# Order of TensorE's work in an attention kernel: both slots' scores ahead of the products with the values, in quads whose scores are corrected by VectorE

## The reference

```
q, k, v = n @ Wq, n @ Wk, n @ Wv              # n = layernorm(x)
latent = (k + v) @ W_down_kv
k_rec, v_rec = latent @ W_up_k, latent @ W_up_v
scores = clip(qh @ kh.T / (sqrt(128) + 1e-8))  # per head, 1024 x 1024
scores = clip(scores * exp(-0.0001 * |i - j|))
out = softmax(scores) @ vh
x = x + out @ Wo
x = x + (float8(layernorm(x)) @ float8(kernel)) * scales + bias
```

## Time and profile before

| | us |
|---|---|
| median of 3 runs (526.9, 526.92, 529.14) | 526.92 |
| the profiled execution's own time | 526.96 |
| its span, first to last instruction | 525.2 |
| TensorE (PE) busy | 487.2 (93%) |
| ScalarE (ACT) busy | 489.5 (93%) |
| VectorE (DVE) busy | 276.8 (53%) |
| GpSimd (POOL) busy | 218.9 (42%) |

### The profile page before, as it was taken

One profiled execution on the slowest core, in us unless ns is written; L12 is line 12 of the kernel. 1 busy time (PEld: TensorE's weight loads), 2 busy tenths in 40 slices (PEclk: granted clock), 3 DMA queues, 4 the chain that ended last, 5 costly groups with the idle time before them and its releaser, 6 DMA issues.

```text
span 525.2 us, 9404 instructions
## 1 busy us (share of the span) xinstructions
PE 487.2 (93%) x3457; PEld 111.9 (21%) x3457; DVE 276.8 (53%) x641; ACT 489.5 (93%) x534; POOL 218.9 (42%) x285
## 2 busy tenths in 40 slices
PE   8799999999999999999999999999999999999961
PEld 3312111122122122122121211122121212121220
DVE  5524554556654654546645565454654564445646
ACT  3789999999999999999999999999999999999961
POOL 0889519791630249982450219993101121002110
PEclk9999999999999999999999999999999999999995
DMA  5589989947994103667976001747987000100000
GB/s 178 166 258 227 325 190 198 338 179 175 258 207 105 46 7 143 210 229 171 249 166 150 8 5 61 275 165 208 259 168 182 8 4 7 47 0 2 1 21 25
DMA packets 50467, 73.79 MB, mean 140 GB/s; under 512 B 6192, under 2 KB 29168, under 8 KB 50416
## 3 DMA queue, kind: packets, MB, share of 16 engines
q1 hardware_dynamic: 49600, 72.85, 50.5%
q10 hardware_dynamic: 816, 0.28, 0.2%
HBM read 35.40 MB, written 35.65 MB: 135 GB/s over the span
## 4 chain that ended last, share of the span: by engine, by line
PE 55%; ACT 31%; issue 7%; DVE 6%; DVEq 0%; ACTq 0%
ACT probs L760 30%; PE ps L960 27%; PE ps L944 16%; DVE ps L1183 3%; PE ps L828 2%; PE ps L824 2%; PE ps L940 2%; PE ps L833 1%; PE ps L861 1%; PE ps L856 1%; PE ps L799 1%; PE ps L868 0%; DVE xn L1231 0%; PE ps L818 0%; DVE stats L1099 0%
## 5 line engine op out<-in xcount | busy, mean ns | idle before, releaser
L760 ACT ACTIVATE probs<-ps 128x1024 f32<-128x1024 f32 x512 | 478.9, 1061 | 9.7 <-DVE ps L1183 6.1
L960 PE MATMUL ps<-probs,V 128*9 128x512 f32 x2048 | 267.8, 594 | 3.2 <-ACT probs L760 0.8
L1183 DVE TENSOR_TENSOR ps<-ps,consts 128x256 f32<-128x256 f32 (+1 forms) x256 | 144.3, 566 | 173.1 <-PE ps L944 166.0
L944 PE MATMUL ps<-Qs,Ks 64*128 64x512 bf16 x992 | 179.1, 385 | 13.8 <-ACT probs L760 7.2
L944 PEld LDWEIGHTS ps<-Qs,Ks 64*128 64x128 bf16 x992 | 42.7, 93 | 281.5 <-ACT probs L760 265.9
L960 PEld LDWEIGHTS ps<-probs,V 128*9 128x9 f32 x2048 | 31.3, 88 | 80.3 <-issue 60.4
L564 POOL TENSOR_SCALAR rs<-mv 128x4 f32<-128x4 f32 (+1 forms) x10 | 2.3, 229 | 102.7 <-DVEq L1365 102.2
L1191 DVE COPY pv_out<-ps 105x512 f32<-105x512 f32 x31 | 21.4, 692 | 33.9 <-PE ps L960 33.9
L647 POOL TENSOR_TENSOR xs<-xs,magic 128x512 f32<-128x512 f32 x7 | 8.9, 1277 | 70.4 <-DVE magic L1244 70.4
L598 POOL TENSOR_TENSOR sq<-sq,parts 128x1024 f32<-128x1024 f32 (+1 forms) x16 | 28.4, 1773 | 1.3
L600 POOL TENSOR_TENSOR parts<-sq,parts 128x1024 bf16<-128x1024 f32 (+1 forms) x16 | 28.3, 1771 | 1.3
(11 more groups left out here) (148 smaller groups left out, 281.4 us busy)
## 6 DMA issues: line engine op xcount, KB each, us to landing
Qs<-qp_dram SPq DMA_DIRECT2D x26, 512.0 KB, 9.5
qp_dram<-parts SPq DMA_DIRECT2D x14, 768.0 KB, 5.2
Ks<-kp_dram SPq DMA_DIRECT2D x26, 384.0 KB, 6.0
kp_dram<-parts SPq DMA_DIRECT2D x12, 384.0 KB, 3.6
kp_dram<-parts SPq DMA_DIRECT2D x6, 768.0 KB, 4.4
qp_dram<-parts SPq DMA_DIRECT2D x7, 512.0 KB, 6.6
X<-L_attn_x SPq DMA_DIRECT2D x10, 256.0 KB, 3.1
Qs<-qp_dram SPq DMA_DIRECT2D x10, 256.0 KB, 9.4
```

The source lines that it names most:

```text
L760: nc.scalar.activation(probs[:, quad % RING, 2 * jp:2 * jp + 2, :].rearrange("p j n -> p (j n)"), ps_all[:, bank * CH:(bank + 2) * CH], AC ...
L944: last = nc.tensor.matmul(bank, Ks[half, g, jp, key_cols(v, kc)], Qs[half, g, jp, qh, v, :], start=True, stop=True)
L960: last = nc.tensor.matmul(pv[32 * j:32 * j + VW, :], V[:, unit // 2 * NB + kc, HG * j + g, :], probs[:, quad % RING, j, :], start=i == 0, ...
L1183: nc.vector.tensor_tensor(own, own, factors, ALU.mult).then_inc(fixed, 1)
```

## The change

In quads whose scores are corrected, the product of quad - 2 is issued after the scores of the second slot and no longer between the two slots. Uncorrected quads keep their order. No instruction is added or removed.

```
                     qk(s)
-                    if quad >= 2 and s % 2 == in_f32:
+
+                    if quad >= 2 and s % 2 == (in_f32 or variant(quad)[1] is not None):
                         weigh(quad - 2)
```

## The result

| | before | after |
|---|---|---|
| median us (runs) | 527.65 (4) | 537.71 (4) |
| lowest, highest | 526.9, 529.14 | 537.54, 537.85 |
| profiled execution, its span | 526.96, 525.2 | 537.85, 536.0 |

The ratio is 1.0185, 95% interval [1.0168, 1.0202]: slower, by 10.1 us by the medians and by 10.9 us between the two profiled executions.

A forecast was written before the change was run, and what follows sets the result against it. Took ScalarE's exponentials, 0.917 us apart, plus stalls from TensorE's side jobs as the bound. Stall terms 20.5 + 1.7 + 0.8 + 1.4 = 24.4 us replace 13.6: 526.96 + 10.8 = 537.8 us, range 532 to 542.

The forecast's parts named there:

- 33 separate long jobs: Lone TensorE side jobs (keys, queries, values, norms, spread sums, projections): late scores stall ScalarE 0.62 us each, 20.5 us.
- 4 long jobs behind a long job: Long jobs in the very next corrected quad: TensorE needs 4.10 us against 3.67, 0.43 us lost each, 1.7 us.
- 6 transposes T: Transposes of input rows on TensorE, step taken as 0.6 us: 0.13 us lost each, 0.8 us in all.
- copies and row moments on VectorE: VectorE's copy waits for a later product, delaying wide corrections: 0.2 us in each of seven units, 1.4 us.
- short jobs and the rest: Short TensorE jobs, 0.51 and 0.33 us to the next scores: lateness nearly or fully forgiven, nothing counted.
- b': Second corrected slot of the quad after a job: old order loses 0.41 us wide, 0.14 narrow; new order forgives it.
- c, d and a': Uncorrected quad's two slots, then the next corrected quad's first: after a long job, old order just forgives their lateness.
- Clean quads cost nothing: In quads without a job, TensorE's idle time and ScalarE's pace cover the moved product: all lateness forgiven.
- (1): Rival: the product's new place costs nothing and corrected second slots' 10.2 us of stalls go: 516.8 us, chance 0.07.
- (2): Rival: each long job costs only TensorE's own overload, 0.43 us: +2.3, 529.3 us, chance 0.06.
- (3): Rival: 30 VectorE copies wait for later products ahead of corrections, 0.2 us more each: 543.8 us, chance 0.05.
- (4): Rival: idle waits drop TensorE's clock to half, one unit so costing 38 us: 576 us, chance 0.02.

The follow-up runs named there:

- e4: The changed kernel, but in corrected quads with a side job the job goes ahead of the moved product: 536.94 us, ratio 1.0157.
- e2: The kernel before, with the product moved only in the 63 corrected quads without any job: 529.79 us, ratio 1.0026.
- e1: The kernel before, with the product moved only in the 36 corrected quads that have a long job themselves: 543.34 us, ratio 1.028.
- e3: The kernel before, with the product moved only in the 37 corrected quads directly behind a quad with a long job: 526.03 us, ratio 0.9972.
- e7: e3 plus, in each group's uncorrected second quad, the product ahead of both slots' scores: 525.03 us against 528.35 before, ratio 0.9918.
- e6: The changed kernel with two extra 512-column matmuls in each of the 14 short jobs: 541.89 us, ratio 1.0241.
- e10: The kernel before, with only VectorE's reciprocal of the sums moved from quad 7 to quad 8 of a unit: 530.62 us, ratio 1.0035.
- e9: e7 with VectorE's reciprocal of the sums moved from quad 7 to quad 8 of a unit: 521.58 us, ratio 0.9864.
- e8: The kernel before, with only the product ahead of both slots' scores in the second quad of each group: 527.61 us, ratio 0.9975.

## Why the prediction was right

**The point, 537.8, against 537.71; the ratio's interval around it.** The agreement of the point is closer than the terms deserve. It adds 10.8 us to one fast execution of the kernel before; its four runs have a median of 527.65, from which the change is 10.1. By the ends of the 512 exponentials in the trace (each step less 0.917; a job's share is what falls on the four slots after it) the 24.4 us that were forecast split like this:

| term | forecast | measured |
|---|---|---|
| 33 separate long jobs | 20.5 (0.62 each) | 20.9 (0.63 each) |
| 4 long jobs behind a long job | 1.7 | 1.4 |
| 6 transposes T | 0.8 | 1.2 |
| copies and row moments on VectorE | 1.4 | 0.5 (0.07 in each of 7 units) |
| short jobs and the rest | 0 | 0.4 |
| sum | 24.4 | 24.4 |

The main term was right in mechanism and size: the separate long jobs cost 0.58 to 0.67 in most places (0.38 four times, behind the norms, and 0.99 in three; e4 brings two of these three down to 0.61), and behind the same jobs it was 0.33 on average in the old order. The value taken for VectorE was nearly three times too high, those for the transposes and the short jobs were too low, and the errors cancel. That the sum meets the measured 24.4 to the tenth is luck. The main term is more than that: the rows above repeat its walk instant by instant, and the job shown there cost 0.67. But its 0.63 is an average over 0.38 to 0.99.

Two workings of the prediction don't hold as they stand. The old order's stalls behind long jobs were forecast as those of b' alone, 10.2 us; they were 12.3, because c, d and a' were "just forgiven" on paper and d and a' were not quite. And the range prices all 37 long jobs at 0.5 and 0.68 and at the lower end adds the 1.7 for the four chained ones once more. With 33 the price gives 16.5 + 1.7 - 13.6 = +4.6 and 22.4 + 1.7 + 0.8 + 1.4 - 13.6 = +12.7, and the measured 10.1 lies inside that too.

**That b' stops stalling** was right: corrected second slots lost 8.6 us before and nothing after (-0.1, within the rounding of the pace). **Clean quads cost nothing** was right in the full change (period 3.67). It doesn't carry over to a kernel that moves only some products: in e2 a moved clean quad makes the copy later, and the next corrected quad, in the old order, loses 0.2 to 0.4 us. **Where it goes back**: the first and second slots of uncorrected quads (c and d) lost 0.0 and 2.7 us before and lose 7.9 and 12.3 after; the first slots of corrected quads (a') went from 2.4 to 4.3. e1 and e3 separate the two sides of the edit: the payment sits in the quads that have the job, the gain in the quads behind them. Units 1 to 5 grew by 1.3 to 2.1 us (forecast: from some 60.5 to 62 or 63) and units 6 and 7 by 0.8 each (forecast: less than 1.2).

**The rivals.** (1), only the gain: it is real, 8.7 us in the corrected second slots of the full change, and the same quads give and take. (2), only the overload of TensorE: the chained jobs cost 0.34, near its 0.43; the separate ones 0.63. (3), VectorE: e4 and the 0.07 a unit speak against it for the full change; in the mixed orders e2 and e3 the copy did cost 7.1 and 4.2 us. (4), the clock: 1.00 from the start to 512 us, with a wait of 0.46 us or more before the second scores of the clean quads, so the loss feared there didn't come. (In the kernel before it was full until 511 us, and not only until 504 as the prediction reads it.)

## What to carry to other kernels

When an engine runs in order and its work waits on gates, an item between two gated ones fills a wait. Moving it behind both turns the wait idle, and the next queue item that is already near its limit pays. Write for each consumer how late its input may start, walk the order once without and once with the odd job, and compare lateness with the limit: here it gave the loss to within 1 us, where shares of busy time say nothing. An edit that helps in one place and hurts in another, by the same condition, is worth splitting: the full change lost 10 us, its good third won 1.5 to 1.9, and with two neighbouring edits 6.8. Where a split gains less than it should, look for what the moved item releases: e3 won 7.3 us in one place and lost 4.2 at the copy, until e7 moved the copy's product too.

## What the runs showed that I had not expected

- The kernels in the old order vary from run to run far more (526.71 to 532.86 in 29 runs of the kernel before) than the changed one (537.54 to 537.85 in 4; e1, e4 and e6 within 1.4 us in 6 each). Six profiles show a transfer of gathered rows 0.7 to 4.4 us late at one reciprocal that stands ahead of corrections on VectorE; those of the slower kernels, which reach it 2 to 3 us later, show none. Moving it 1.8 us later narrowed the spread to 1.3 us (e10) and 2.9 us (e9, where it still waited 0.5). Why the transfer's landing differs between executions is open.
- Moving that reciprocal cost 2.3 us in the old order and next to nothing in e9. The traces put the difference on the product behind it, 1.45 to 1.59 us beside GpSimd's work in e10 and 0.69 in e9. A small shift of one engine can so bring two others together; no run tests this by itself.
- The wait for the copy costs 1.0 us in the kernel before and at most 0.5 in the changed one, but 7.1 us more than before in e2 and 4.2 more in e3. Two edits that look apart (e3 and e8, 1.5 and 1.3 us by their ratios) gave 4.3 together in e7.
